# Maxima and u turned in 32x32 blocks on VectorE, u stored by SyncE, and a tail with another order and early loads

## The chip, the cores and the metric

One core of a Trainium2 chip runs the whole program. The metric is the device time in microseconds (us). The engines named here are TensorE (PE in the rows; its weight loads are PEld), VectorE (DVE), ScalarE (ACT), GpSimd (POOL) and SyncE (SP), which only issues transfers. Each works through its own list of instructions in order, and waits on semaphores that the others raise.

## The reference

A layer of a perceiver on 32 batches of 64 tokens with 128 features. Cross attention over a context of 1601 rows per batch, causal self attention over the tokens of a batch, and a gated feed-forward part with quantised weights and activations:

```python
# cross attention: 16 heads of 64, per batch b
qh = rms_norm(layernorm(x) @ Wq); kh = rms_norm(ctx @ Wk)
scores = where(arange(1601) < len[b], qh @ kh.T / sqrt(64), -1e9)
x = x + (softmax(scores) @ (ctx @ Wv)) @ Wo
# self attention: 16 heads of 64, causal mask (64 tokens lie within the global part of the mask)
x = x + (softmax(q @ k.T / sqrt(64)) @ v) @ w_out
# feed-forward, with the largest magnitude of whole tensors as quantisation scales
x = x + qdq(silu(qdq(z @ Wg.T)) * qdq(z @ Wu.T)) @ qdq(Wd).T
```

## The kernel before

**Three parts in a row.** `cross_attention` (to 2188 us in the profile), `self_attention` (to 2477) and `ffn`. A barrier of all engines lies between two parts.

**Cross attention.** The queries are first carried through Wk, so that a score is a product of the query with the raw context; the keys are still computed, for their norms. Then comes a loop over batches p, each of 13 steps c, one per tile of 128 context rows (the last has 65). `each_step` writes the steps out for the first and last batches and as a hardware loop between; `draining(p)` is p >= 32, where no new batch begins. One step of TensorE is: `project` (keys of a tile 11 ahead, for the sum of squares), `turn` (a transpose of the raw tile 12 ahead into the PSUM bank x_ps), `score` (two halves), `values` (tile of an earlier batch, LAG steps behind, times its probabilities, into u_ps), and at the end of some steps transposes that belong to a batch as a whole.

**Maxima.** VectorE keeps `best`, the maximum over the 13 score tiles element by element (128 x 1024, `keep_best`, not in step 1). When a batch is whole, the maximum over the 128 partitions is wanted, as one row of 1024. TensorE turns `best` in two groups of four 128x128 transposes (`turn_best`, end of steps 0 and 1), VectorE reduces each group from PSUM (`best_of_columns`, steps 1 and 2), TensorE turns the result (`turn_row`, step 2), ScalarE copies it (`save_row`, step 3), SyncE stores it to DRAM as `best_rows` and loads it back broadcast to all partitions as `best_all` (`spread_best`, step 6 of SyncE's own list, which runs about three steps ahead of TensorE). GpSimd subtracts it from the scores (`shift`), ScalarE exponentiates.

**u.** When all 13 tiles of values are summed, VectorE inverts the sums of probabilities (`invert_sums`, step LAG), ScalarE divides (`divide`), TensorE turns the result in two groups of four (`turn_u`, end of steps 7 and 8), ScalarE copies each group out of x_ps (`save_uT`) and issues one transfer of 128 rows of 4 KB to the DRAM tensor ut (`store_uT`).

**Stage.** Raw context tiles are loaded into `stage`, four buffers and one for the short tile, by SyncE (`load_stage`), each when the tile before it in its buffer has been turned. SyncE's transfers go through one queue in the order in which they are issued.

**Self attention.** STEPS run from -10 to 15, one token tile of 128 (two batches) per step, with five stages at different leads: `sum_heads` (tile i+10, 64 small products of u with Wv Wo, from the transfer `load_u` of 1 MB per tile into two buffers), `turn_y` (tile i+9), `project_qk` (part of the q and k projections, a group of four tiles in four steps, i from -5 to 10), `project_v`, `score`, and `turn_p`, `mix` for tile i. Of VectorE's work the chain for y is: add, variance, (ScalarE: rough root), `normalise`, then, when TensorE has turned y and ScalarE has copied it, yT_lo = y - yT_hi. The feed-forward weights are quantised by VectorE in one piece at step -6.

Of the kernel before, what the change touches and what calls it, by code (L numbers as in the profile page):

```python
# [110 lines left out]
def arena_views(arena):  # L111

    def at(first, count):
        return arena[:, first * HL:(first + count) * HL]

    return {"wqkv": at(0, 3), "wv": at(3, 1), "wo": at(4, 1), "wout": at(5, 1), "wvo": at(6, 2), "wvo2": at(8, 2),
            "wvT": at(10, 1), "wv2T": at(11, 1), "qk": [at(10, 8), at(18, 8)], "v2": [at(0, 2), at(2, 2)],
            "pT": at(4, 1), "p": at(5, 1)}
# [22 lines left out]
LAG = 6  # L141
# [42 lines left out]
def cross_attention(nc, sem, ident, x, ctx_in, Wq, Wk, q_norm_w, k_norm_w, lens, qs, best_rows, ut_out,  # L184
                    arena, Wv, Wo, w_qkv, w_out):
# [11 lines left out]
    UW = D + 1  # L197
    with ExitStack() as ctx:
# [20 lines left out]
        best_row = sb("best_row", [P, G])  # L219
        row_sb = sb("row_sb", [G, P])  # L220
# [46 lines left out]
        q_in, rows_in, ut_stored = sem("q_in"), sem("rows_in"), Turns(sem("ut_stored"), 1, 16)  # L267
# [19 lines left out]
        best_turned = Turns(sem("best_turned"), 2, 2)  # L287
        best_row_ready = Turns(sem("best_row_ready"), 2, 2)
        row_turned = Turns(sem("row_turned"), 2)
# [3 lines left out]
        last_spread, last_best_ready = sem("last_spread"), sem("last_best_ready")  # L293
# [4 lines left out]
        u_turned = Turns(sem("u_turned"), 2, 2)  # L298
        uT_ready = Turns(sem("uT_ready"), 2, 2)
# [14 lines left out]
        def _(sp):  # L314
# [29 lines left out]
            def spread_best(b):  # L344
                sp.wait_ge(row_saved.sem, row_saved.ended(b))
                sp.dma_start(best_rows[bass.ds(b, 1), :].rearrange("b (g p) -> (b g) p", p=P),
# [31 lines left out]

            row_stored.start(sp)
# [12 lines left out]
            sp.wait_ge(ut_stored.sem, ut_stored.ended(B - 1))  # L392
# [64 lines left out]
        def _(act):  # L457
# [95 lines left out]
            def save_row(b):  # L553
                act.wait_ge(row_turned.sem, row_turned.ended(b))
                act.wait_ge(row_stored.sem, row_stored.ended(b - 1))
                act.activation(row_sb[:, :], x_ps[0:G, 0:P], ACT.Copy).then_inc(row_saved.sem, 1)

            def save_last_best(b):
                for h in range(2):
                    act.wait_ge(last_spread, h + 1)  # L560
                    act.activation(best_all[:, (b % 2) * HL + h * HALF:(b % 2) * HL + (h + 1) * HALF], k_ps[h][:, :],
                                   ACT.Copy).then_inc(last_best_ready, 1)

            def divide(b):
                for k in range(3):
# [7 lines left out]
            def save_uT(b, h):  # L573
                act.wait_ge(u_turned.sem, u_turned.ended(b, h + 1))
                act.wait_ge(ut_stored.sem, ut_stored.ended(b - 1))
                act.activation(uT_sb[:, half(h)], x_ps[:, :], ACT.Copy).then_inc(uT_ready.sem, 1)  # L576

            def store_uT(b):
                act.wait_ge(uT_ready.sem, uT_ready.ended(b))
                act.dma_start(ut_out[bass.ds(b, 1), :, :].rearrange("b d n -> (b d) n"),  # L580
                              uT_sb[:, :]).then_inc(ut_stored.sem, 16)
# [39 lines left out]
            for turns in (hi_ready, squared, logged, y0_ready, probs_ready, row_saved, u_ready, uT_ready,  # L621
                          ut_stored, q_hi_ready):
# [1115 lines left out]
```

## Time and profile before

| | us |
|---|---|
| median of 3 runs (2638.5 to 2650.76) | 2642.37 |
| the profiled execution | 2639.05 |
| its span, first to last instruction | 2637.3 |

| stretch, us | what | TensorE busy | VectorE busy | clock granted |
|---|---|---|---|---|
| 0 to 151 | queries, first tiles | 116.25 | 97.00 | 0.93 |
| 151 to 2128 | loop over batches | 1957.83 | 1692.01 | 1.00 |
| 2128 to 2188.5 | drain, weight products | 49.10 | 31.86 | 0.97 |
| 2188.5 to 2477 | self attention | 234.85 | 140.69 | 0.90 |
| 2477 to 2637.3 | feed-forward | 68.38 | 104.25 | 0.72 |

A row of the timeline gives the start in us, the duration, engine, line of the kernel, operation, output and inputs; in brackets stands the idle time of that engine before it and what ended it. Matmuls overlap, so the distance between two starts tells more than a duration. The clock is TensorE's, as a share of 2.4 GHz.

### The profile page before, as it was taken

To read this page: it belongs to the slowest core of one execution; us is meant where nothing else is said; L and a number is where in the kernel's file an instruction comes from. 1 tells how busy PE (TensorE), PEld (TensorE's weight loads), DVE (VectorE), ACT (ScalarE), POOL (GpSimd) and SP (SyncE) were. 2 spreads that over 40 slices of the span, in tenths; PEclk is the share of its full clock that TensorE was granted. 3 is DMA by queue.
4 is the path that set the end of the run, shared out by engine and by line. 5 is a ranking of instruction groups with operands and counts; after the bars stand their busy time and mean duration, and the time that the engine had idled before them with its cause. 6 is when DMAs were issued, how large, how long until landed. Compare 5 with 4: busy or idle time off the path is not lost. (4 is left out here: it accounts for less than half of the span.)

```text
span 2637.3 us, 54923 instructions
## 1 busy us (share of the span) xinstructions
PE 2426.4 (92%) x17271; PEld 2036.6 (77%) x17271; DVE 2065.8 (78%) x3185; ACT 1333.0 (51%) x2659; POOL 1168.1 (44%) x605
## 2 busy tenths in 40 slices
PE   6879999999999999999999999999999986788852
PEld 3657888888888888888888888888888886565522
DVE  6789888888888888888888888888888863355757
ACT  4644555555555555555555555555555542334540
POOL 3403555555555555555555555555555510001155
PEclk8999999999999999999999999999999998988975
DMA  2421111111111211111111111111111115210000
GB/s 86 160 100 43 50 50 52 55 54 54 49 50 51 60 50 50 49 58 50 49 50 50 49 49 50 49 58 50 57 50 50 45 65 173 69 50 1 2 0 16
DMA packets 141723, 144.97 MB, mean 55 GB/s; under 512 B 10520, under 2 KB 120272, under 8 KB 141520
## 3 DMA queue, kind: packets, MB, share of 16 engines
q1 hardware_dynamic: 137040, 127.16, 15.3%
q10 hardware_dynamic: 4608, 16.78, 1.6%
q8 instruction: 51, 0.84, 0.1%
q14 instruction: 24, 0.20, 0.0%
HBM read 109.17 MB, written 34.73 MB: 55 GB/s over the span
## 5 line engine op out<-in xcount | busy, mean ns | idle before, releaser
L404 POOL TENSOR_TENSOR probs<-arena,best_all 128x1024 f32 (+2 forms) x398 | 944.9, 2377 | 918.9 <-DVE best L765 918.9
L984 PEld LDWEIGHTS u_ps<-rows,probs 128*128 128x128 f32 x6656 | 806.5, 192 | 47.1 <-issue 5.3
L984 PE MATMUL u_ps<-rows,probs 128*128 (+1 forms) x6656 | 810.1, 275 | 9.0 <-ACT probs L597 6.6
L750 DVE SCALAR_TENSOR_TENSOR arena<-s_ps,mask,rrms 128x512 f32 (+2 forms) x832 | 618.8, 745 | 249.6 <-PE s_ps L853 249.4
L597 ACT ACTIVATE probs<-probs 128x1024 f32<-128x1024 f32 (+1 forms) x416 | 439.6, 1058 | 512.9 <-POOL probs L404 501.5
L550 ACT ACTIVATE squares<-k_ps 128x512 f32<-128x512 f32 (+1 forms) x832 | 462.8, 595 | 191.4 <-PE k_ps L853 128.0
L726 DVE TENSOR_REDUCE ssq<-squares 128x16 f32<-128x1024 f32 (+1 forms) x416 | 502.4, 1208 | 0.0
L765 DVE TENSOR_TENSOR best<-best,arena 128x1024 f32<-128x1024 f32 (+1 forms) x352 | 468.9, 1332 | 0.3
L851 PE MATMUL k_ps<-w_hi,cT_hi 128*128 128x512 f32 (+1 forms) x832 | 363.2, 437 | 12.9 <-DVE cT_lo L720 12.9
L851 PE MATMUL s_ps<-q_hi,cT_hi 128*128 (+2 forms) x832 | 362.0, 435 | 2.5 <-ACT uT_sb L576 1.4
L853 PE MATMUL s_ps<-q_hi,cT_lo 128*128 (+2 forms) x832 | 327.8, 394 | 0.0
L853 PE MATMUL k_ps<-w_hi,cT_lo 128*128 128x512 f32 (+1 forms) x832 | 327.6, 394 | 0.0
L852 PE MATMUL s_ps<-q_lo,cT_hi 128*128 (+2 forms) x832 | 327.6, 394 | 0.0
L852 PE MATMUL k_ps<-w_lo,cT_hi 128*128 128x512 f32 (+1 forms) x832 | 326.9, 393 | 0.0
L851 PEld LDWEIGHTS s_ps<-q_hi,cT_hi 128*128 128x128 f32 (+1 forms) x832 | 153.6, 185 | 59.8 <-ACT uT_sb L576 1.9
L851 PEld LDWEIGHTS k_ps<-w_hi,cT_hi 128*128 128x128 f32 (+1 forms) x832 | 154.1, 185 | 41.7 <-DVE cT_lo L720 19.9
L853 PEld LDWEIGHTS k_ps<-w_hi,cT_lo 128*128 128x128 f32 (+1 forms) x832 | 152.9, 184 | 39.5
L853 PEld LDWEIGHTS s_ps<-q_hi,cT_lo 128*128 128x128 f32 (+1 forms) x832 | 152.8, 184 | 39.4
L852 PEld LDWEIGHTS k_ps<-w_lo,cT_hi 128*128 128x128 f32 (+1 forms) x832 | 154.5, 186 | 19.9
L852 PEld LDWEIGHTS s_ps<-q_lo,cT_hi 128*128 128x128 f32 (+1 forms) x832 | 154.3, 186 | 20.0
L720 DVE TENSOR_TENSOR cT_lo<-x_ps,cT_hi 128x128 fp32r<-128x128 f32 (+1 forms) x416 | 114.8, 276 | 45.2 <-ACT cT_hi L544 45.2
L576 ACT ACTIVATE uT_sb<-x_ps 128x512 f32<-128x512 f32 x64 | 38.4, 599 | 154.1 <-PE x_ps L970 154.1
(222 smaller groups left out, 2312.8 us busy)
## 6 DMA issues: line engine op xcount, KB each, us to landing
stage<-in_ctx SPq DMA_DIRECT2D x384, 64.0 KB, 1.8
rows<-in_ctx SPq DMA_DIRECT2D x32, 768.0 KB
queries<-probs SPq DMA_DIRECT2D x16, 1024.0 KB, 4.0
q_plain<-queries SPq DMA_DIRECT2D x32, 512.0 KB, 3.4
u_transposed<-uT_sb ACTq DMA_DIRECT2D x32, 512.0 KB, 2.7
a_uT<-u_transposed SPq DMA_DIRECT2D x16, 1024.0 KB, 4.9
best_all<-best_rows SPq DMA_DIRECT2D x31, 512.0 KB, 3.6
arena<-in_L_attn_w_qkv SPq DMA_DIRECT2D x1, 1536.0 KB, 6.6
```

The source lines that it names most:

```text
L404: pool.tensor_tensor(probs[0:r, slot_of(c, PRING), :], scores_at(b, c), best_all[0:r, bass.ds((b % 2) * HL, HL)], ALU.subtract).then_inc(s ...
L550: act.activation(squares[0:rows_of(c), half(h)], k_ps[h][0:rows_of(c), :], ACT.Square).then_inc(squared.sem, 1)
L576: act.activation(uT_sb[:, half(h)], x_ps[:, :], ACT.Copy).then_inc(uT_ready.sem, 1)
L597: act.activation(tile, tile, ACT.Exp).then_inc(probs_ready.sem, 1)
L720: dve.tensor_tensor(cT_lo[:, c, 0:r], x_ps[:, 0:r], cT_hi[:, c, 0:r], ALU.subtract).then_inc(lo_ready.sem, 1)
L726: dve.tensor_reduce(ssq[0:r, c * H:(c + 1) * H], squares[0:r, :].rearrange("p (h d) -> p h d", d=HD), AX_X, ALU.add).then_inc(summed.sem, 1)
L750: dve.scalar_tensor_tensor(out=scores_at(p, c, h * HALF, HALF).rearrange("p (h l) -> p h l", l=L), in0=s_ps[h][0:r, :].rearrange("p (h l) ...
L765: dve.tensor_tensor(best[0:r, :], so_far, scores_at(p, c), ALU.max).then_inc(kept.sem, 1)
L851: pe.matmul(out, cT_hi[:, c, 0:r], hi, start=True, stop=False)
L852: pe.matmul(out, cT_hi[:, c, 0:r], lo, start=False, stop=False)
L853: return pe.matmul(out, cT_lo[:, c, 0:r], hi, start=False, stop=True)
L984: last = pe.matmul(u_ps[g // 3][:, at:at + UW], probs[0:r, s, g * P:(g + 1) * P], rows, start=(c == 0 and g % 3 == 0), stop=(c == NC - 1), ...
```

## The change

In the loop, VectorE transposes `best` in 32x32 blocks into u_sb (`turn_blocks`, end of step 1), reduces each block's rows (`best_of_blocks`, steps 2 and 3, from SBUF, 128x32 results), TensorE turns the result at the end of step 4, and VectorE reduces the four rows groups of that from PSUM into `row_sb` of 32x32 (`best_of_groups`, step 5). TensorE's groups for `best` and ScalarE's `save_row` are gone. u is transposed in 32x32 blocks by VectorE too (`turn_u`, a quarter of 128x256 in each of four steps); blocks then lie in the wrong place, and SyncE's store puts them right: four transfers, each of 32 partitions x 32 pieces of 32 numbers (128 B). The last batch keeps the old way for both (`turn_last_best`, `turn_last_u`). LAG goes from 6 to 7.

In the tail, six u tiles (U_EARLY) are loaded into the finished half of the score buffer during the drain; `project_qk` waits only for the group's own tiles and takes the whole wait before its fourth product; `sum_heads` waits for one copy less of each kind; VectorE makes yT_lo before it normalises the next tile; the weights are quantised in three parts, at steps -7, -6 and -5.

```diff
-LAG = 6
+LAG = 7
+SIDE = 32
+            def store_uT(b):
+                sp.wait_ge(uT_ready.sem, uT_ready.ended(b))
+                dest = ut_out[bass.ds(b, 1), :, :].rearrange("b (c i) (g q k) -> b q i g c k", i=SIDE, k=SIDE, q=P // SIDE)
+                for q in range(P // SIDE):
+                    sp.dma_start(dest[:, q, :, :, :, :].rearrange("b i g c k -> (b i) g c k"),
+                                 uT_sb[q * SIDE:(q + 1) * SIDE, :].rearrange("i (g c k) -> i g c k", k=SIDE, c=D // SIDE)
+                                 ).then_inc(ut_stored.sem, 16)
+            def load_u_early(t):
+                sp.wait_ge(shifted.sem, shifted.ended((B - 1) * NC + 2 * t + 1))
+                if t == 0:
+                    sp.wait_ge(ut_stored.sem, ut_stored.ended(2 * U_EARLY - 1))
+                else:
+                    sp.wait_ge(u_early_in, 16 * t)
+                load_u(sp, w_now["uT"][t], ut_out, t, u_early_in)
 # SyncE's step
+                if c == NC - 1 and on.finish and not ending(p):
+                    store_uT(p - 2)
+                if draining(p) and (p - B) * NC + c in range(9, 9 + 2 * U_EARLY, 2):
+                    load_u_early(((p - B) * NC + c - 9) // 2)
 # ScalarE
             def divide(b):
+                act.wait_ge(uT_ready.sem, uT_ready.ended(b - 1))
+                act.wait_ge(best_row_ready.sem, best_row_ready.ended(min(b + 1, B - 2) if isinstance(b, int) else b + 1))
-                if on.rows and c == 3 and not draining(p):
-                    save_row(p - 1)
-                if on.finish and c in (LAG + 2, LAG + 3):
-                    save_uT(p - 2, c - LAG - 2)
-                if on.finish and c == LAG + 4:
-                    store_uT(p - 2)
 # VectorE
+            def turn_blocks(b):
+                dve.wait_ge(kept.sem, kept.ended(b))
+                dve.wait_ge(uT_ready.sem, uT_ready.ended(b - 2))
+                dve.transpose(u_sb[:, :], best[:, :]).then_inc(blocks_turned.sem, 1)
+            def best_of_blocks(b, h):
+                ...
+                dve.tensor_reduce(best_row[:, cols], u_sb[:, half(h)].rearrange("p (j k) -> p j k", k=SIDE),
+                                  AX_X, ALU.max).then_inc(best_row_ready.sem, 1)
+            def best_of_groups(b):
+                dve.wait_ge(row_turned.sem, row_turned.ended(b))
+                dve.wait_ge(row_stored.sem, row_stored.ended(b - 1))
+                dve.tensor_reduce(row_sb[:, :], x_ps[0:BLOCKS, 0:P].rearrange("j (g i) -> j i g", i=SIDE),
+                                  AX_X, ALU.max).then_inc(row_saved.sem, 1)
+            def turn_u(b, k):
+                if k == 0:
+                    dve.wait_ge(u_ready.sem, u_ready.ended(b))
+                    dve.wait_ge(ut_stored.sem, ut_stored.ended(b - 1))
+                cols = slice(k * HL // 4, (k + 1) * HL // 4)
+                dve.transpose(uT_sb[:, cols], u_sb[:, cols]).then_inc(uT_ready.sem, 1)
 # TensorE's step
-                if on.rows and c in (0, 1) and not draining(p):
-                    turn_best(p - 1, c)
-                if on.rows and c == 2 and not draining(p):
+                if on.rows and c == 4 and not draining(p):
                     turn_row(p - 1)
-                if on.finish and c in (LAG + 1, LAG + 2):
-                    turn_u(p - 2, c - LAG - 1)
+                if c in (LAG + 1, LAG + 2) and ending(p):
+                    turn_last_u(p - 2, c - LAG - 1)
 # tail: SyncE, VectorE, TensorE
-            load_u(0)
             sp.dma_start(x1[:, :].rearrange("p (t d) -> p t d", d=D),
                          x.rearrange("b l d -> (b l) d").rearrange("(t p) d -> p t d", p=P)).then_inc(x_in, 16)
-            load_u(1)
+            for t in range(U_EARLY, U_EARLY + 2):
+                load_u(sp, uT[:, t % 2, :], ut, t, uT_in[t % 2])
-                if i == -6:
-                    dve.wait_ge(ffn_w_in, 48)
-                    quantize_weights(dve, link, ffn_w, ws, ffn_w_ready)
+                if -7 <= i < -4:
+                    if i == -7:
+                        dve.wait_ge(ffn_w_in, 48)
+                    quantize_weights(dve, link, ffn_w, ws, i + 7, ffn_w_ready)
-                pe.wait_ge(v_saved, 4 * upto(i - 1, V_AHEAD))
-                pe.wait_ge(qk_saved, parts_upto(i - 1))
+                pe.wait_ge(v_saved, max(0, 4 * upto(i - 1, V_AHEAD) - 1))
+                pe.wait_ge(qk_saved, max(0, parts_upto(i - 1) - 1))
             def project_qk(j, r, i):
-                pe.wait_ge(yT_lo_ready, upto(i, TURN_Y_AHEAD))
+                pe.wait_ge(yT_lo_ready, 4 * j + 4)
...
+                    if k == 3:
+                        pe.wait_ge(yT_lo_ready, upto(i, TURN_Y_AHEAD))
```

What this does to the order of instructions, at three places. First VectorE in step 1 of a batch and the start of step 2 (written-out part); best is the running maximum, ssq the sums of squares, ms their mean, x_ps the bank that TensorE turns into. Before:

```order
L750 SCALAR_TENSOR_TENSOR arena<-s_ps,mask,rrms 128x512
L726 TENSOR_REDUCE ssq<-squares 65x16
L732 TENSOR_SCALAR ms<-ssq 128x64
L770 TENSOR_REDUCE best_row<-x_ps 128x4
L765 TENSOR_TENSOR best<-arena 128x1024
```

And of the change:

```order
L780 SCALAR_TENSOR_TENSOR arena<-s_ps,mask,rrms 128x512
L756 TENSOR_REDUCE ssq<-squares 65x16
L800 STREAM_TRANSPOSE u_sb<-best 128x1024
L762 TENSOR_SCALAR ms<-ssq 128x64
L795 TENSOR_TENSOR best<-arena 128x1024
```

The reduction from x_ps has gone from the start of step 2, and the block transpose of the whole maximum stands at the end of step 1, ahead of the next batch's first maximum.

Second SyncE at the end of the loop's body, from the load of tile 11 on; the branch goes back to the load of the next batch's tile 0. Before:

```order
L318 DMA stage<-in_ctx 128x128
L317 REGISTER_ALU
L318 ISA [waits turned]
L318 DMA stage<-in_ctx 65x128
L161 REGISTER_ALU
L161 COMPARE_AND_BRANCH
```

And of the change:

```order
L333 DMA stage<-in_ctx 65x128
L369 ISA
L372 ISA [waits uT_ready]
L372 DMA u_transposed<-uT_sb 256x4x32
L372 ISA
L372 DMA u_transposed<-uT_sb 256x4x32
L372 ISA
L372 DMA u_transposed<-uT_sb 256x4x32
L372 ISA
L372 DMA u_transposed<-uT_sb 256x4x32
L175 REGISTER_ALU
L175 COMPARE_AND_BRANCH
```

A wait for VectorE's last quarter of uT and four transfers stand ahead of the loads of the next batch's tiles.

Third VectorE in a tail step, from the sums of the softmax on (a_inv) to the sum with the attention's output (x<-a_ov). Before:

```order
L1291 RECIPROCAL a_inv<-a_total 128x16 [waits a_normed,a_links]
L1266 TENSOR_TENSOR a_y_stat<-a_y_stat 128x1 [waits a_y_rough,a_y_turned]
L1267 SCALAR_TENSOR_TENSOR a_y_stat<-a_y_stat 128x1 [waits a_links]
L1268 SCALAR_TENSOR_TENSOR a_y_stat<-a_y_stat 128x1 [waits a_links]
L1269 TENSOR_SCALAR a_y<-x_then_z,a_y_stat 128x128 [waits a_links]
L1320 TENSOR_TENSOR a_yT_lo<-a_work,a_yT_hi 128x128 [waits a_yT_ready]
L1324 TENSOR_TENSOR x<-a_ov,x_then_z 128x128 [waits a_mixed]
```

And of the change:

```order
L1346 RECIPROCAL a_inv<-a_total 128x16 [waits a_normed,a_links]
L1367 TENSOR_TENSOR a_yT_lo<-a_work,a_yT_hi 128x128 [waits a_yT_ready]
L1321 TENSOR_TENSOR a_y_stat<-a_y_stat 128x1 [waits a_y_rough,a_y_turned]
L1322 SCALAR_TENSOR_TENSOR a_y_stat<-a_y_stat 128x1 [waits a_links]
L1323 SCALAR_TENSOR_TENSOR a_y_stat<-a_y_stat 128x1 [waits a_links]
L1324 TENSOR_SCALAR a_y<-x_then_z,a_y_stat 128x128 [waits a_links]
L1380 TENSOR_TENSOR x<-a_ov,x_then_z 128x128 [waits a_mixed]
```

a_yT_lo, which the projection of q and k waits for, now comes before the four instructions that normalise the next tile.

## Rows read from the trace of the kernel before

**Rows 1.** Busy time by stretch: core, then as headed (the clock is PEclk).

```profile
core 0: us, PE busy (x) PEld busy (x) DVE busy (x) ACT busy (x) POOL busy (x), PEclk, DMA share, GB/s
1000.00:2060.00 1060.00, 1060.00 (x6663) 925.96 (x6662) 902.31 (x1305) 580.15 (x1148) 560.61 (x236) 1.00 0.16 51
...
2320.00:2340.00 20.00, 16.93 (x230) 12.01 (x229) 10.62 (x25) 8.06 (x17) 1.91 (x1) 0.84 0.16 53
...
2440.00:2460.00 20.00, 19.41 (x271) 12.00 (x264) 12.94 (x31) 12.66 (x26) 3.80 (x2) 1.00 0.01 2
```

**Rows 2.** Timeline of TensorE in the loop; stage is turned in step 1 of two batches.

```profile
1009.94 1.95 PE L984 MATMUL u_ps<-rows,probs 128*128 x16
...
1011.64 0.48 PE L851 MATMUL k_ps<-w_hi,cT_hi 128*128 128x512 f32 x1
...
1014.62 1.95 PE L984 MATMUL u_ps<-rows,probs 128*128 x16
...
1016.76 0.48 PE L851 MATMUL k_ps<-w_hi,cT_hi 128*65 128x512 f32 x1
...
1018.23 0.27 PE L926 MATMUL x_ps<-ident,stage 128*128 128x128 f32 x1
...
1080.97 0.27 PE L926 MATMUL x_ps<-ident,stage 128*128 128x128 f32 x1
```

**Rows 3.** Timeline of VectorE in the loop: end of step 11; steps 4 to 6.

```profile
1006.55 1.21 DVE L726 TENSOR_REDUCE ssq<-squares 128x16 f32<-128x1024 f32 x1
...
1036.61 1.21 DVE L765 TENSOR_TENSOR best<-best,arena 128x1024 f32<-128x1024 f32 x1
...
1038.63 0.75 DVE L750 SCALAR_TENSOR_TENSOR arena<-s_ps,mask,rrms 128x512 f32 x1 [0.81 <-PE s_ps L853]
```

**Rows 4.** Timeline of the transfers that SyncE issues.

```profile
1029.17 0.32 SPq L346 DMA_DIRECT2D best_rows<-row_sb  x1
...
1030.83 0.35 SPq L350 DMA_DIRECT2D best_all<-best_rows  x1
...
1043.36 0.40 SPq L366 DMA_DIRECT2D rows<-in_ctx  x1
```

**Rows 5.** Timeline of GpSimd: its first subtraction of a batch.

```profile
1038.30 2.38 POOL L404 TENSOR_TENSOR probs<-arena,best_all 128x1024 f32 x1 [2.59 <-DVE best L765]
```

**Rows 6.** Busy time by stretch, amid the load of rows1; last: DMA share, GB/s.

```profile
1046.25:1046.50 0.25, 0.25 (x3) 0.21 (x2) 0.25 (x1) 0.18 (x1) 0.00 (x0) 1.00 1.16 352
```

**Rows 7.** The page, part 6: transfers, count, KB each, median us to landing.

```profile
u_transposed<-uT_sb ACTq DMA_DIRECT2D x32, 512.0 KB, 2.7
...
best_all<-best_rows SPq DMA_DIRECT2D x31, 512.0 KB, 3.6
```

**Rows 8.** Timeline of TensorE in the tail.

```profile
2193.46 6.31 PE L1356 MATMUL a_work<-arena,a_uT 128*64 128x128 f32 x64 [6.16 <-DMA a_uT<-u_transposed]
...
2225.64 0.30 PE L1381 MATMUL a_work<-ident,a_y 128*128 128x128 f32 x1 [3.46 <-DVE a_yT_lo L1320]
...
2241.03 0.50 PE L1394 MATMUL a_tp<-a_yT_hi,a_wqk_hi 128*128 128x512 f32 x1 [2.69 <-DVE a_yT_lo L1320]
...
2244.97 3.71 PE L1356 MATMUL a_work<-arena,a_uT 128*64 128x128 f32 x64 [0.89 <-ACT arena L1240]
...
2251.63 0.50 PE L1394 MATMUL a_tp<-a_yT_hi,a_wqk_hi 128*128 128x512 f32 x1 [2.69 <-DVE a_yT_lo L1320]
...
2339.53 0.80 PE L1394 MATMUL a_tp<-a_yT_hi,a_wqk_hi 128*128 128x512 f32 x1 [3.07 <-DVE a_yT_lo L1320]
...
2359.91 0.80 PE L1394 MATMUL a_tp<-a_yT_hi,a_wqk_hi 128*128 128x512 f32 x1 [3.08 <-DVE a_yT_lo L1320]
...
2440.07 0.50 PE L1394 MATMUL a_tp<-a_yT_hi,a_wqk_hi 128*128 128x512 f32 x1
...
2451.04 0.50 PE L1394 MATMUL a_tp<-a_yT_hi,a_wqk_hi 128*128 128x512 f32 x1
```

**Rows 9.** Waits, 2188 to 2460 us: us in total, times, longest.

```profile
PE a_tp L1394 <- DVE a_yT_lo L1320: 37.7, 12, 5.3
```

More of the change, by code:

```diff
@@ L117, in arena_views, with load_u, ending @@
             "wvT": at(10, 1), "wv2T": at(11, 1), "qk": [at(10, 8), at(18, 8)], "v2": [at(0, 2), at(2, 2)],
-            "pT": at(4, 1), "p": at(5, 1)}
+            "pT": at(4, 1), "p": at(5, 1), "uT": [at(NC + 2 * t, 2) for t in range(U_EARLY)]}
+U_EARLY = 6
+def load_u(sp, dest, ut, t, done):
+    sp.dma_start(dest.rearrange("p (b n) -> p b n", b=2), ut[2 * t:2 * t + 2, :, :].rearrange("b d n -> d b n")).then_inc(done, 16)
+def ending(p):
+    return isinstance(p, int) and p == B + 1
 class On:
@@ L620, in _ @@
             act.preload_act_table_set(EXP_LN)
[L621 to L622 removed]
+            for turns in (hi_ready, squared, logged, y0_ready, probs_ready, u_ready, q_hi_ready):
                 turns.start(act)
@@ L790, in step @@
                 n = p * NC + c
-                if on.rows and c in (1, 2) and not draining(p):
-                    best_of_columns(p - 1, c - 1)
+                if on.rows and c == 5 and not draining(p):
+                    best_of_groups(p - 1)
                 if on.rows and c == 1 and draining(p):
@@ L811, in step @@
                     sum_squares(n + KEYS_AHEAD, at_step(p, c, KEYS_AHEAD)[1])
+                if on.rows and c == 1 and not draining(p):
+                    turn_blocks(p - 1)
+                if on.rows and c in (2, 3) and not draining(p):
+                    best_of_blocks(p - 1, c - 2)
+                if on.finish and LAG < c <= LAG + 4 and not ending(p):
+                    turn_u(p - 2, c - LAG - 1)
                 if on.early and c == NC - 3:
@@ L833, in save_wvo @@
                                         ).then_inc(wvo_saved, 1)
-            for turns in (lo_ready, summed, ms_ready, rrms_ready, scaled, kept, best_row_ready, inv_ready):
+            for turns in (lo_ready, summed, ms_ready, rrms_ready, scaled, kept, blocks_turned, best_row_ready, row_saved,
+                          inv_ready, uT_ready):
                 turns.start(dve)
@@ L1015, in step @@
                     project(n + KEYS_AHEAD, at_step(p, c, KEYS_AHEAD)[1])
-                if on.rows and c in (1, 2) and not draining(p):
-                    pe.wait_ge(best_row_ready.sem, best_row_ready.ended(p - 1, c))
-                if on.rows and c == 3 and not draining(p):
+                if on.rows and c == 5 and not draining(p):
                     pe.wait_ge(row_saved.sem, row_saved.ended(p - 1))
-                if on.finish and c in (LAG + 2, LAG + 3):
-                    pe.wait_ge(uT_ready.sem, uT_ready.ended(p - 2, c - LAG - 1))
+                if c == LAG + 2 and ending(p):
+                    pe.wait_ge(last_saved, 3)
                 if on.turn:
@@ L1041, in step @@
                     spread_last_best(p - 1)
-                if on.finish and c in (LAG + 1, LAG + 2):
-                    turn_u(p - 2, c - LAG - 1)
-            for turns in (turned, keys, scored, valued, best_turned, row_turned, u_turned):
+                if c in (LAG + 1, LAG + 2) and ending(p):
+                    turn_last_u(p - 2, c - LAG - 1)
+            for turns in (turned, keys, scored, valued, row_turned):
                 turns.start(pe)
@@ L1187, in _ @@
             sp.dma_start(ffn_w[:, 2 * FF:3 * FF], w_down).then_inc(ffn_w_in, 16)
-            for t in range(2, TILES):
-                load_u(t)
+            for t in range(U_EARLY + 2, TILES):
+                sp.wait_ge(summed, t - 1)
+                load_u(sp, uT[:, t % 2, :], ut, t, uT_in[t % 2])
         @block.gpsimd
@@ L1310, in step @@
                     softmax_sums(t)
+                t = i + TURN_Y_AHEAD
+                if 0 <= t < TILES:
+                    dve.wait_ge(yT_ready, t + 1)
+                    at = t % 8 * P
+                    dve.tensor_tensor(yT_lo[:, at:at + P], work[1][:, 0:P], yT_hi[:, at:at + P], ALU.subtract).then_inc(yT_lo_ready, 1)
                 t = i + SUM_AHEAD
```

139 lines of the change are left out of this document (71 added, 68 removed).

## The prediction

> **What bounds the kernel now.** I read the busy time by stretch first, then the timelines of TensorE and VectorE inside the loop, then the tail's timeline and its waits. In 1000 to 2060 us TensorE is busy for all of it, at a granted clock of 1.00 (2.4 GHz), while VectorE has 902 of 1060 us and GpSimd 561 [rows 1]. VectorE is the one that waits, as for the 0.81 us before the scores at 1038.63 [rows 3]. So the loop over batches costs what TensorE is given, 62.74 us per batch (1018.23 to 1080.97, the same turn of the same tile) [rows 2]. The tail is different: at 2320 to 2340 the clock is 0.84, at 2440 to 2460 it is 1.00 [rows 1], and in the first TensorE stands still for 3.07 us in every step before projecting q and k, waiting for VectorE's yT_lo [rows 8]; 12 such waits make 37.7 us [rows 9].
>
> **The change, part by part, the loop.** TensorE loses four groups of four transposes per batch (maxima in steps 0 and 1, u in steps 7 and 8); the single turn of the row stays. Without a group the time from a step's values to the next projection is 1.70 us (1009.94 to 1011.64), with one it is 2.14 (1014.62 to 1016.76) [rows 2]: 0.44 us each, all on the path, since TensorE waits for nothing there. The maxima of 31 batches are turned so (the last batch's stay on TensorE), 62 groups; u has as many, of which the last two lie in the drain, where TensorE is not the bound, and I leave those out: 60. 122 x 0.44 = 53.7 us less.
>
> VectorE gains, per batch, a block transpose of 128x1024, four of 128x256 and a small reduction of 32x128; two PSUM reductions of 128x512 become two in SBUF, which I price alike. No row shows a transpose on VectorE. From above I bound the large one by 2.38 us, what GpSimd needs over 1024 columns [rows 5]; from below by the 0.75 us that VectorE needs over 512 [rows 3]. I take 1.2, by its reduction and its maximum over 1024 columns (1.21 us each [rows 3]), and 0.3 for a quarter. That adds 1.2 + 4 x 0.3 + 0.2 = 2.6 us to 902 / 1060 of 62.74 = 53.4; 56.0 of the new 61.0 fit (62.74 - 4 x 0.44 = 60.98). So it stays off the path only if the work lies evenly. Step by step: after a plain step VectorE is done at 1037.82 and waits 0.81 us for the next scores [rows 3], so a step gives back 0.8 us of lateness. Step 1 has no maximum and takes most of the large transpose free. By adding up, step 2 starts its scaling 0.4 us late, then holds a reduction and the refinement; step 3 starts about 1.0 late. TensorE wants cT_lo, which comes behind the first scaling, about 1.0 us after it is normally there (an estimate from the order of the two timelines). I book 0.1 us per batch, none to 1.0.
>
> A second small one: maxima now reach the row in step 5, not 3. Today the row's store is issued at 1029.17, the broadcast at 1030.83 [rows 4], and it lands 3.6 us later [rows 7], near 1034.4; GpSimd first uses it at 1038.30 [rows 5]. In the new order it is stored about 1.6 us into step 5, so lands 5.3 us after that, some 2.3 us into step 6, where GpSimd (now a step later) wants it at 2.2. ScalarE's exponential, its division and then cT_hi sit behind that chain. I book 0.2, none to 1.0 where the row's 32 pieces are slower than its 8. Together 0.3 x 31 = 9 us more; with a transpose of twice the price, about 1.5 x 31 = 47.
>
> **The store of u.** SyncE writes it as four transfers of 1024 pieces of 128 B instead of one of 128 rows of 4 KB. They stand ahead of the next three stage loads on its queue, and SyncE itself waits for the last transpose there. The first of those loads used to have three steps in hand. VectorE's sum of step 11 ends at 1007.76 [rows 3]; with a quarter transpose and some lateness uT is whole near 1008.5, pieces move from about 1009.7 (an estimate: 1.1 us or so behind the issue, as the load of rows1 issued at 1043.36 was under way well before 1046.25). The tile is turned at 1018.23 less one removed group, 1017.8, and I allow 1 us behind the last piece, so the 4096 pieces have 7.1 us, 1.73 ns each [rows 2, 4, 6]. Price of a piece: no row has it. Pieces of 512 B moved at 352 GB/s in that load [rows 6], 1.45 ns each, 6.0 us in all. By bytes alone it would be 2.7, the landing time of the old store [rows 7]. Upwards the rows give no end (the row's store, 8 pieces in 1.66 us, is all latency [rows 4]), and I cap it at two 512 B pieces per piece, 12.0 us. I take 6.0 to 7.5, by the nearest row, and book nothing; at the cap the stall is 4.9 us per batch, 150 us.
>
> The Trainium skill (DMA: Bandwidth & Descriptors, Specifications) speaks against this edit: it puts the least transfer for line rate at 512 B and says that below it the engine reads, modifies and writes. By that rule a piece pays for two passes, and with the second rival's length the sum would be its 2680. No row of this trace shows such a store, and the sum above goes by the row.
>
> **The tail.** Six of the sixteen u tiles are loaded while the drain runs. Today TensorE waits 6.16 us for the first and then works slowly; step 0's add falls about 6 us earlier, bounded now by x, which moves to the front of the queue. Quantising the weights in one piece kept TensorE for 3.46 us (2225.64); in thirds behind the normalisation it still delays two adds by about 1.3 us each. With the wait for yT_lo and the slow clock of that step I get 6.5 us. Then the wait itself: three of four projections need only tiles turned a step earlier, and take 2.1 us at full clock; yT_lo now comes before the normalisation, so by adding up it is there about 2.5 us after the sum of heads, when the fourth wants it. Steps with all parts take 20.4 us (2339.53 to 2359.91). Steps without y and without a wait take 10.97 (2440.07 to 2451.04); adding the sum of heads (3.7) gives 14.7, and with the turn of y and the smaller pauses I keep 14.6 to 15. Six such steps: 35 us. The two steps of 10.6 (2241.03 to 2251.63) go to 6.9: 7. Three others (before, between and after) about 5 each: 15. All: 6 + 6.5 + 35 + 7 + 15 = 70 us [rows 8]. 36 of these are the waits, most of the rest is the clock: behind the pause the projection's row has 0.80 us (2339.53), where it has 0.50 without one (2440.07). If the clock stays low regardless only about 48 come. I take 60. VectorE has 10.6 us of work in 20 [rows 1], one step; that fits 14.6.
>
> LAG 7 moves one tile of values out of the loop into the drain, where it takes as long as it did; early loads share the queue with u's store. I book 0, +-5.
>
> **Sum.** The profiled execution took 2639.05 us (span 2637.3 and 1.75 around it): 2639.05 - 53.7 + 9 - 60 = 2534. The median of the runs shown is 3.3 above it, so 2538.
>
> **Rivals.** (1) The store is somewhat slower than the queue allows, 1.8 to 2.6 ns a piece: a stall of 0.3 to 3.6 us in each of 30 batches, 2545 to 2640. For it: writes, scattered, in four transfers; against: a piece carries a quarter of the bytes of the row that I price it by. Chance 0.23. (2) The other side: the same mechanism beyond 3.7 us per batch (decided at 2.65 ns a piece, since 53.7 + 60 - 9 = 105 us is what must be used up with the drain; at 12.0 us of transfer, 4.9 x 30 = 147) gives about 2680, slower. TensorE would show the wait at the stage's turn in step 1. Chance 0.15. (3) VectorE becomes the bound: a transpose of twice the price, or blocking with GpSimd, 1.5 us per batch, 2538 + 38 = 2576, up to 2600. For it: VectorE's small reserve; against: the transposes come 2.7 us after the maxima, when GpSimd's 2.38 us are over. Chance 0.15. (4) The tail does not do what it says, because another semaphore holds the projection: 2538 + 50 = 2588. Chance 0.05. Forecast: 0.42.
>
> **Numbers.** 2538 us. Its own range is 2515 to 2560; with (1), (3) and (4) it becomes 2512 to 2635, leaving out case (2) and little at the lower edge. Within 0.5% is 2629 to 2656, about what a measurement of this kernel can tell from no change; it gets the upper edge of (1) and the lower of (2), 0.05. Faster 0.82, slower 0.13.
>
> **What would show it.** A period of 61.0 to 61.5 us between the same turns; no TensorE wait for a stage load; a block transpose of 1.1 to 1.3 us; the store landing in under 9 us; in the tail steps of about 14.6 us at a clock near 1.00, with yT_lo waits below 1 us. A period above 62.7, or a wait of TensorE on the stage, makes it wrong; a tail step that keeps a 3 us pause makes that term wrong.

## The result, and the profile after

The changed kernel takes 2530.51 us (median of 4 runs, 2528.97 to 2531.81), the kernel before 2641.75 beside it: a ratio of 0.9573, 95% interval 0.9549 to 0.9598. 2538 was forecast, with 2512 to 2635 as the range. Single executions of 4165 to 8387 us, which came up beside the rest with the kernel before as with changed ones, are left out of every ratio.

The profiled executions have spans of 2637.3 and 2527.2 us, so 110.1 us went. A short tile is the last one of a batch, with 65 rows; TensorE turns one in each batch. Cut at the same instructions in both timelines, the 110.1 us went here:

| stretch | before | after | less |
|---|---|---|---|
| start to the first turn of a short tile | 150.67 | 149.58 | 1.1 |
| from there to the last tile's key projection (2083.16, 2039.60) | 1932.49 | 1890.02 | 42.5 |
| from there to the end of the weight products (2187.30, 2139.48) | 104.14 | 99.88 | 4.3 |
| from there to the sum of heads of step -5 (2218.47, 2169.24) | 31.17 | 29.76 | 1.4 |
| steps -5 to 0 (to 2291.14, 2217.87) | 72.67 | 48.63 | 24.0 |
| steps 0 to 5 (to 2391.83, 2289.16) | 100.69 | 71.29 | 29.4 |
| from there to the end | 245.5 | 238.0 | 7.4 |

Busy time by stretch, of the changed kernel; it answers to [rows 1]. Columns are as there.

```profile
1000.00:2060.00 1060.00, 1057.13 (x6533) 914.82 (x6532) 968.48 (x1435) 566.20 (x1114) 575.61 (x243) 1.00 0.20 51
2232.12:2246.38 14.26, 14.26 (x230) 10.39 (x230) 10.85 (x26) 7.73 (x18) 1.90 (x1) 1.00 0.22 76
```

In the loop TensorE is still busy nearly all the time, VectorE has 968 us instead of 902. The second row is one full step of the tail: 14.26 us, TensorE never idle, the granted clock 1.00, where it stood at 0.84 in 2320 to 2340 before. Five full steps (0 to 5) as a whole, before and then after:

```profile
2291.14:2391.83 100.69, 85.32 (x1147) 60.09 (x1146) 53.64 (x126) 40.32 (x86) 9.53 (x5) 0.85 0.13 43
```

```profile
2217.87:2289.16 71.29, 71.29 (x1146) 51.95 (x1146) 54.26 (x126) 38.67 (x86) 9.53 (x5) 1.00 0.18 61
```

In steps -5 to 0 TensorE had 50.42 us of work in 72.67, at a clock of 0.91, and has 45.60 in 48.63 at 1.00. So of the 53.4 us that went in steps -5 to 5, 34.6 were time in which TensorE stood idle, and 18.8 are the same products done faster.

TensorE in the loop, against [rows 2]: stage turned in step 1 of two batches, and in steps 7 and 8 between them.

```profile
1061.23 0.27 PE L988 MATMUL x_ps<-ident,stage 128*128 128x128 f32 x1
...
1089.53 0.27 PE L988 MATMUL x_ps<-ident,stage 128*128 128x128 f32 x1
...
1094.57 0.27 PE L988 MATMUL x_ps<-ident,stage 128*128 128x128 f32 x1
...
1122.61 0.27 PE L988 MATMUL x_ps<-ident,stage 128*128 128x128 f32 x1
```

The period here is 61.38 us. From short tile to short tile the 29 whole periods run from 61.10 to 61.53, mean 61.26, where before they ran from 62.70 to 62.76, mean 62.73 (62.74 in the rows). The unevenness is new, and the rows show one place of it: 5.04 us from step 7 to step 8. Averaged over 20 batches, the time from the turn of one step to the turn of the next is:

| step | 0 | 1 | 2 | 3 | 4 | 5 | 6 | 7 | 8 | 9 to 12 |
|---|---|---|---|---|---|---|---|---|---|---|
| before | 5.11 | 5.10 | 4.79 | 4.67 | 4.69 | 4.69 | 4.75 | 5.12 | 5.10 | 4.67 to 4.69 |
| after | 4.69 | 4.67 | 4.67 | 4.68 | 4.80 | 4.80 | 4.69 | 4.88 | 4.67 | 4.67 to 4.69 |

A plain step takes 4.67. The four groups are gone whole (0.43 each). The 0.12 in step 4 is the turn of the row, which stood in step 2 before; what the new order costs stands in steps 5 (0.11) and 7 (0.20), and step 6 gives 0.06 back.

VectorE's new instructions: engine, count, ns min/median/max, first and last start (two lines of the source).

```profile
L800 DVE STREAM_TRANSPOSE u_sb<-best x31: 1229/1231/1236, 209.0 to 2044.5; 128x1024 f32<-128x1024 f32 x31
...
L826 DVE STREAM_TRANSPOSE uT_sb<-u_sb x124: 425/435/440, 301.8 to 2113.4; 128x256 f32<-128x256 f32 x124
```

The store of u, against [rows 4, 6, 7]: SyncE's issues, then two stretches of the share of the queue (last: DMA share, GB/s), then the page's part 6.

```profile
1052.18 3.01 SPq L372 DMA_DIRECT2D u_transposed<-uT_sb  x4
1055.73 2.08 SPq L333 DMA_DIRECT2D stage<-in_ctx  x4
```

```profile
1053.00:1053.50 0.50, 0.50 (x4) 0.36 (x3) 0.50 (x1) 0.50 (x2) 0.00 (x0) 1.00 0.01 1
...
1053.50:1055.50 2.00, 2.00 (x19) 1.95 (x18) 2.00 (x5) 0.37 (x2) 1.24 (x1) 1.00 0.98 169
```

```profile
best_all<-best_rows SPq DMA_DIRECT2D x31, 512.0 KB, 3.8
u_transposed<-uT_sb SPq DMA_DIRECT2D x124, 128.0 KB, 2.5
```

The pieces start 1.3 us behind the first issue and fill the 16 engines at 169 GB/s, so the 524 KB take 3.1 us: 0.76 ns for a piece of 128 B. They are over near 1056.6, and the tile that comes first behind them is turned at 1061.23 without a wait. The old store, rows of 4 KB in the same direction, ran at 394 GB/s once under way:

```profile
1026.60:1027.40 0.80, 0.80 (x6) 0.68 (x5) 0.77 (x3) 0.38 (x2) 0.10 (x1) 1.00 0.96 394
```

TensorE in the tail, against [rows 8]: the sums of heads of steps -10, -9 and 1, and the fourth product of two steps.

```profile
2140.96 3.71 PE L1417 MATMUL a_work<-arena 128*64 128x128 f32 x64 [1.48 <-PEq L213]
2148.54 6.15 PE L1417 MATMUL a_work<-arena 128*64 128x128 f32 x64 [3.87 <-DVEq L1358]
...
2211.28 0.50 PE L1457 MATMUL a_work<-a_yT_hi,a_wqk_hi 128*128 128x512 f32 x1 [0.77 <-DVE a_yT_lo L1367]
...
2232.12 3.71 PE L1417 MATMUL a_work<-arena,a_uT 128*64 128x128 f32 x64
...
2309.22 0.50 PE L1457 MATMUL a_work<-a_yT_hi,a_wqk_hi 128*128 128x512 f32 x1 [1.08 <-DVE a_yT_lo L1367]
```

And TensorE's waits in 2140 to 2400, us in total, times, longest; the last of these answers to [rows 9].

```profile
PE a_work L1417 <- DVEq L1358: 6.2, 5, 3.9
...
PE a_work L1457 <- DVE a_yT_lo L1367: 2.8, 3, 1.1
```

37.7 us of waits for yT_lo have become 2.8. What is left at the front is the add of x (L1358 of VectorE) that the second sum of heads waits for.

### The profile page after: what moved, and what is told of

It reads as the page before. It is cut to its first block and busy times, and to the rows that moved or that the text cites. A ratio compares the mean times of both kernels' runs of the same rounds, so it can differ in the third digit from the quotient of the medians.

```text
span 2527.2 us, 54183 instructions
## 1 busy us (share of the span) xinstructions
PE 2358.9 (93%) x16775; PEld 1966.5 (78%) x16775; DVE 2149.5 (85%) x3384; ACT 1282.4 (51%) x2566; POOL 1165.3 (46%) x604
## 5 line engine op out<-in xcount | busy, mean ns | idle before, releaser
L586 ACT ACTIVATE squares<-k_ps 128x512 f32<-128x512 f32 (+1 forms) x832 | 455.4, 591 | 126.2 <-PE k_ps L915 67.0
L795 DVE TENSOR_TENSOR best<-best,arena 128x1024 f32<-128x1024 f32 (+1 forms) x352 | 475.6, 1351 | 0.1
L580 ACT ACTIVATE cT_hi<-x_ps 128x128 fp32r<-128x128 f32 (+1 forms) x416 | 115.5, 278 | 0.0
```

The lines of the kernel that those rows point to most:

```text
L580: act.activation(cT_hi[:, c, 0:rows_of(c)], x_ps[:, 0:rows_of(c)], ACT.Copy).then_inc(hi_ready.sem, 1)
L586: act.activation(squares[0:rows_of(c), half(h)], k_ps[h][0:rows_of(c), :], ACT.Square).then_inc(squared.sem, 1)
L795: dve.tensor_tensor(best[0:r, :], so_far, scores_at(p, c), ALU.max).then_inc(kept.sem, 1)
```

## The experiments

Each is the changed kernel with one edit, or with those that its heading names. The time from the start to the first short tile is between 149.2 and 159.0 us in these profiles, with the same code there, so small effects are read as the time between two instructions, not from the medians alone.

**1. The tail as it was, the loop changed** (all the tail's hunks of the diff undone).

> The changed kernel with the tail as it was: whole wait for yT_lo ahead of the projection, yT_lo behind the normalisation, weights quantised in one piece, no early loads of u, sum_heads' waits as before. The loop keeps its change. Theory (the two parts add up): from the end of the weight products to the end of the program the traces differ by 62 us (450.0 against 387.7), so this kernel takes 2530.5 + 62 = 2593 us, steps of 20.4 us in the tail. Rival (early loads and the loop's stores of u disturb each other, so that part of the tail's gain is used up in the loop or the drain): clearly under 2593, 2580 or less.

Measured 2593.65 us; ratio to before 0.9815, 0.9787 to 0.9843. The loop alone is worth 47.5 us (2641.19 beside it), the tail 63.1, and they add up. Steps 1 to 3 take 20.37 to 20.45 us again.

**2. The wait alone.**

```diff
 def project_qk(j, r, i):
-                pe.wait_ge(yT_lo_ready, 4 * j + 4)
+                pe.wait_ge(yT_lo_ready, upto(i, TURN_Y_AHEAD))
```

> The changed kernel, only the projection of q and k waits for the newest yT_lo ahead of its first product instead of ahead of its fourth. Theory: in a full step yT_lo is there at 2238.8 where the projection begins at 2237.76, so TensorE waits 1.1 us in each of some 11 steps: 12 to 13 us, 2543, if only the wait itself counts. Rival (the granted clock falls behind such a pause, as it stood at 0.84 in the old steps with their 3.07 us pause): steps of 17 us or more instead of 15.4, in all 30 us or more, 2560, and a clock below 0.95 in the steps 2240 to 2330.

Measured 2558.03 (2550.36 to 2565.2). Since the start varies, the time from the first sum of heads to the end is surer: 413.6 us against 386.2, 27.4 more. Busy time of this kernel in steps -5 to 0 and 0 to 5:

```profile
2242.79:2319.79 77.00, 72.70 (x1147) 52.30 (x1146) 54.26 (x126) 40.38 (x86) 9.53 (x5) 1.00 0.16 57
...
2178.24:2242.79 64.55, 51.48 (x554) 38.23 (x554) 23.43 (x73) 22.56 (x54) 1.91 (x1) 0.89 0.19 66
```

Both theories hold, each in its part. In the full steps TensorE stands still for 0.86 us a step, each costs 1.14 us (15.40 against 14.26), and the clock stays at 1.00. In steps -5 to 0, where TensorE had 51.48 of 64.55 us of work, the clock is 0.89, and these five steps cost 15.9 us more: 10.0 in which TensorE is idle, and 5.9 because the same 554 products take 51.48 us and not 45.60. Another 5.8 us stand in the last full step and the one behind it, at a clock of 0.88.

**3. VectorE's order alone**: yT_lo behind `normalise` again.

> The changed kernel, only VectorE normalises the next tile of y before it makes yT_lo, as it did before; the narrow wait stays. Theory: the normalisation takes 2.4 us of VectorE (2238.72 to 2241.1), so yT_lo comes at about 2241.1 where the fourth product stands at 2239.9: 1.2 us per step, 11 steps, 13 us, 2544. Rival (the fourth product has slack because of ScalarE's copies that project_v waits for, so that the order alone costs nothing): 2531 to 2534. Rival with the clock: as for the front wait, 2560.

Measured 2545.57 (2543.38 to 2548.51), and 398.9 us from the first sum of heads, 12.7 more. The theory's 13 as a sum, with full steps of 15.56 us at a clock of 1.00. They do not lie evenly, as the theory had them: a full step costs 1.3 us, step -1 costs 4.05 by itself, and steps -5 to -2 together 0.8.

**4. Both.**

> The changed kernel with both the old wait and the old order on VectorE, the rest of the tail as changed. Theory: the two hide each other's gain: the wait is 1.1 + 2.4 = 3.5 us a step, more than the sum of both alone, and the clock falls: steps of about 20 us, so 2530.5 + 50 = 2580. Rival (waits only, the clock stays near 1.00): 11 x 3.5 = 38, 2569.

Measured 2587.54; from the first sum of heads 442.6 us, 56.3 more, where the two alone make 40.1. The same two stretches of this kernel:

```profile
2239.40:2338.72 99.32, 83.96 (x1146) 59.34 (x1146) 53.64 (x126) 40.33 (x86) 9.53 (x5) 0.86 0.13 44
...
2170.61:2239.40 68.79, 51.09 (x554) 38.07 (x554) 23.43 (x73) 22.53 (x54) 1.90 (x1) 0.88 0.18 62
```

Now the clock is down in the full steps too: the same 1146 products take 83.96 us of TensorE, where they take 72.70 in experiment 2 and 71.29 in the changed kernel. Waits of 12 times 3.2 us make 38.7 of the 56; the rest goes with the clock.

**5. The weights quantised in one piece**, at step -6.

> The changed kernel with the feed-forward weights quantised in one piece at step -6, ahead of the sums of the softmax, as before. Theory (the prediction's term of 6.5 us; of the two kernels with the old wait and the old order, that with one piece takes 59.2 us from the sum of heads of step -6 to that of step -2 without its own wait for x, that with three parts 53.5 or so): 6 us are lost, 2536, and they stand in the steps -6 to -3. Rival (with the narrow wait the projection no longer needs yT_lo at once, so VectorE's block delays only the adds): 2 us, 2532.

Measured 2531.77 (2531.01 to 2533.79): the rival. Step -5 takes 12.78 us against 8.71, step -6 4.25 against 5.53, and the steps behind them are equal. With the narrow wait the long block costs 2.8 us by these two steps (1.3 by the medians).

**6. No early loads of u** (U_EARLY = 0).

> The changed kernel without the six early loads of u (U_EARLY = 0); u and x are loaded behind the barrier in the old order. Theory (from two earlier traces: with early loads the first sum of heads comes 4.5 us sooner, but then TensorE stands for VectorE's add, which waits for x, and works through its first two tiles at a low clock; from the last turn of a short tile to the sum of heads of step -5 it is 132.8 us with and 134.4 without): 1.5 us are lost, 2532, inside what the medians can tell; in the trace 134 to 135 us between those two points. Rival (the prediction's term): 6 us are lost, 2537, 139 us between the points.

Measured 2534.59; between the two points 135.75 us (2038.75 to 2174.50) against 132.86 in the changed kernel: 2.9 us, nearer to the theory. TensorE waits 6.19 us for the first u tile, as before, but no longer for x behind it:

```profile
2148.45 5.99 PE L1417 MATMUL a_work<-arena,a_uT 128*64 128x128 f32 x64 [6.19 <-DMA a_uT<-u_transposed]
2156.00 3.71 PE L1417 MATMUL a_work<-arena,a_uT 128*64 128x128 f32 x64 [1.56 <-DMA a_uT<-u_transposed]
```

**7. Six tiles of x loaded early as well** (run with the edits of 12; a load into a free slot behind the wait of the first early u load, and VectorE's add reads it there).

> As the kernel before it, and the first six tiles of x loaded early too, into a free slot of the arena during the drain; the add of steps -10 to -5 reads them there. Theory (x is what bounds the tail's start: TensorE stands 3.87 us for the add, and the second tile's sum then takes 6.15 instead of 3.71 us at a low clock): from the end of the weight products to the sum of heads of step -5 it is 31.2 us in the changed kernel and becomes 25, 6 us less, 2512 to 2515. Rival (something else, such as the first u tile or the clock, holds the start as long): 30 us there and 2518 to 2521.

Measured 2517.65 (2515.34 to 2519.79), ratio to before 0.9531, 0.9514 to 0.9547. Its first two sums of heads:

```profile
2132.05 5.38 PE L1426 MATMUL a_work<-arena 128*64 128x128 f32 x64 [3.42 <-PEq L214]
2138.03 3.71 PE L1426 MATMUL a_work<-arena 128*64 128x128 f32 x64 [0.61 <-DVEq L1367]
```

The wait for the add went from 3.87 (4.32 in kernel 12) to 0.61 us, and the second sum is fast. But the first now stands 3.42 us behind TensorE's own sequencer and is slow. From the end of the weight products to step -5, where the theory had 31.2 us (this is the kernel before; the changed kernel has 29.8) and 25 with the early loads, it is 27.68 against 29.46 in kernel 12: 1.8 us, not 6. Another 1.3 us are missing from the drain ahead of it (129.86 against 132.94 from the last short tile's turn to step -5), but the drain varies by as much between kernels that have the same code there. From the first short tile to the end the two kernels differ by 1.1 us; most of the 5.1 us between the medians can be the start, which took 6.9 us longer in the profile of kernel 12. What the 3.42 us are, no run shows; the kernel of experiment 4, which loads no x early, has 2.81 us at the same place.

**8. The store of u issued twice** (the second time to a spare tensor), and **9. three times.**

```diff
+                for to in [dest] + [ut_spare[...] ...]:
                     for q in range(P // SIDE):
-                        sp.dma_start(dest[:, q, ...
+                        sp.dma_start(to[:, q, ...
```

> The changed kernel, every store of u issued twice in the loop (the second four transfers go to a spare tensor in DRAM), so SyncE moves 8192 pieces of 128 B ahead of the next stage loads. In the trace the 4096 pieces move from 1053.3 to about 1056.5, at 153 to 198 GB/s with the 16 engines full: 3.2 us, 0.77 ns a piece. Theory (the prediction's 7.1 us between the start of the pieces and 1 us ahead of the tile's turn): 6.4 us fit, 2530 to 2535. Rival (the reserve is smaller, as the loads behind the store are late already): 3 us per batch, 2620.

> The same with three stores, 12288 pieces. Theory: 9.6 us of transfer against 7.1, so a stall of 2.5 us in each of 30 batches, 75 us, 2605, with TensorE waiting for stage ahead of a turn in step 1. Rival (pieces of two stores overlap better, or later loads take up the delay from the ring of four buffers): under 2560. Rival (other transfers of the batch, rows1 and the row of maxima, are delayed as well): over 2640.

Twice: 2530.89 us (2527.79 to 2532.45), no difference. The queue in its loop:

```profile
1054.25:1060.25 6.00, 6.00 (x43) 5.38 (x43) 5.67 (x9) 2.45 (x6) 3.77 (x2) 1.00 1.02 174
```

At this rate the 8192 pieces (1049 KB) take 6.0 us, and they cost nothing, as 7.1 us of room says. Three times: 2646.34 (2638.06 to 2660.66), 116 us more, mean period 65.3. TensorE waits at the turn of step 1, as the second rival of the prediction had it:

```profile
1049.94 0.33 PE L989 MATMUL x_ps<-ident,stage 128*128 128x128 f32 x1 [2.71 <-DMA stage<-in_ctx]
```

The step ahead of this turn takes 7.63 us on average instead of 4.69, the one behind it 6.04 instead of 4.67. The second of these, 1.4 us, is what the expectation lacked: the next load was late too. So the end of the reserve lies between 6.0 us of transfer and the 9.3 us that 12288 pieces take at 0.76 ns. The wait grew by 2.95 us (7.63 less 4.69), which puts it near 6.4 us (an estimate: 9.3 less 2.95), and behind it a batch pays 4.0 us.

**10. The block transpose of the maxima made twice.**

> The changed kernel, the block transpose of the maxima made twice (the second waits for the first, same result): VectorE has 1.3 us more in step 1 of each batch. Theory (lateness step by step): cT_lo ends at 1068.45 in step 2 and the projection that wants it begins at 1069.11, in step 3 1073.48 against 1073.78; so 0.65 us are lost in step 2 and some 0.35 in step 3, 1.0 us per batch, 31 us, 2561. Rival (VectorE's free share, 5 us of 61, takes it): 2531. Rival (all of it is lost): 1.3 x 31 = 40, 2571.

Measured 2566.01 (2563.73 to 2566.69), 35.5 more. Step 2 takes 5.39 us (0.72 more), step 3 5.03 (0.35), step 4 4.95 (0.15), all others are equal. VectorE's reserve in these steps was about 0.1 us, although it is idle for 9% of the loop. The theory holds, 15% low.

**11. The turned row reduced ahead of the sum of squares**, in step 4 of VectorE.

```diff
-                if on.rows and c == 5 and not draining(p):
-                    best_of_groups(p - 1)
                 ...
+                if on.rows and c == 4 and not draining(p):
+                    best_of_groups(p - 1)
                 if on.keys:
                     sum_squares(...)
```

> The changed kernel, only VectorE reduces the turned row (best_of_groups) ahead of the sum of squares of step 4 instead of at the start of step 5. Theory (the period's 61.26 us are 13 x 4.67 = 60.71 and 0.12 for turning the row, 0.12 for TensorE's wait for the reduction in step 5, and 0.1 to 0.4 in step 7, where the broadcast of the row comes late and holds GpSimd, ScalarE's division, cT_hi, cT_lo and so the projection): both waits go, the period is 60.85 in nearly all batches, 0.4 x 31 = 12 us less, 2518. Rival (only the wait in step 5 goes): 2526. Rival (VectorE waits some 0.4 us for the row in step 4 and that delays the scaling behind it): 2531 or more.

Measured 2531.49 (2524.28 to 2538.89), period 61.13 to 61.26, mean 61.20. A miss. The theory had 60.85. Step 5 fell from 4.80 to 4.68, and GpSimd's waits for best_all (46.5 us in 20 of 21 batches of the changed kernel, 400 to 1700 us) are gone; but step 7 did not fall: it takes 4.95 where it took 4.88 (4.86 to 4.95 in the kernels above that leave the loop's order alone). GpSimd then waits for VectorE's maximum instead. ScalarE in step 7 of this kernel:

```profile
1094.34 1.06 ACT L628 ACTIVATE probs<-probs 128x1024 f32<-128x1024 f32 x1 [1.89 <-POOL probs L440]
1095.31 2.16 ACT L602 ACTIVATE u_sb<-u_ps,inv_sum 128x128 f32<-128x128 f32 x8
1097.31 1.14 ACT L586 ACTIVATE squares<-k_ps 128x512 f32<-128x512 f32 x2
1098.26 0.35 ACT L580 ACTIVATE cT_hi<-x_ps 128x128 fp32r<-128x128 f32 x1
```

The tile was turned at 1095.63, yet cT_hi is made at 1098.26, and the projection starts at 1099.08. So what bounds step 7 in this kernel is this chain on ScalarE, not when the row arrives. Experiment 12 tests it.

**12. The same, and cT_hi ahead of the squares in the step with the division.**

```diff
+                if on.turn and on.finish and c == LAG:
+                    split_hi(n + TURN_AHEAD, at_step(p, c, TURN_AHEAD)[1])
                 if on.keys:
                     for h in range(2):
                         square(...)
-                if on.turn:
+                if on.turn and not (on.finish and c == LAG):
                     split_hi(...)
```

> The changed kernel with the turned row reduced ahead of the sum of squares, and ScalarE copying cT_hi ahead of the squares in the step with the division. Theory (with the first edit alone step 7 still took 4.95 us, since behind the division's 2.16 us ScalarE makes the squares, 1.14, and only then cT_hi, which cT_lo and the next projection wait for): cT_hi comes 1 us earlier, step 7 falls to 4.68, the period from 61.20 to 60.95 or less, against 61.26 that is 9 to 13 us in all, 2518 to 2521. Rival (the squares come late instead, and the projection then waits for the banks k_ps that they read): the period stays at 61.15 to 61.2, 2529. The time from the start to the first short tile varies by some us from run to run, so the period is the surer reading.

Measured 2522.79 (2519.42 to 2525.63), ratio to before 0.9547, 0.9530 to 0.9563; each of its five runs is under the fastest of the changed kernel. ScalarE and TensorE of this kernel in the same step:

```profile
1090.39 2.15 ACT L602 ACTIVATE u_sb<-u_ps,inv_sum 128x128 f32<-128x128 f32 x8
1092.39 0.33 ACT L580 ACTIVATE cT_hi<-x_ps 128x128 fp32r<-128x128 f32 x1
1092.55 1.14 ACT L586 ACTIVATE squares<-k_ps 128x512 f32<-128x512 f32 x2
```

```profile
1090.69 0.27 PE L990 MATMUL x_ps<-ident,stage 128*128 128x128 f32 x1
...
1093.89 0.48 PE L915 MATMUL k_ps<-w_hi,cT_hi 128*128 128x512 f32 x1
```

From the turn to the next projection it is 3.20 us, where kernel 11 needed 3.45. Step 7 takes 4.68, the period is 60.88 to 60.96 in all 29 batches. Both kernels 12 and 7 beat the changed kernel, by 7.7 and 12.9 us in the medians, and by 9.9 and 11.0 from the first short tile to the end; 29 periods shorter by 0.34 make 9.9.

## Why the prediction was right

**TensorE's term, 53.7 us.** Right. A group cost 0.43 us in the table of steps (0.44 booked), and nothing took its place but the loop's losses, which come next.

**The loop's losses, 0.3 us per batch.** The size was right, the two reasons were not, so that the size came out is luck. The period fell by 62.73 - 61.26 = 1.47 us where four groups make 1.76, so the loss is 0.29. None of it is the lateness behind the large transpose, for which I booked 0.1: steps 2 and 3 take 4.67 and 4.68. Experiment 10 shows that this was close, since the next 1.3 us on VectorE are paid nearly in full, and so the upper bound of the term (1.5 us per batch for a transpose of twice the price) was well placed, at 1.2. The other 0.2, for the row that comes late to GpSimd, was seen as a wait (up to 2.6 us in the trace), but experiment 11 took that wait away and step 7 did not get shorter. What the table of steps shows is 0.11 in step 5 (the reduction ahead of cT_lo on VectorE) and 0.2 in step 7 (the division and the squares ahead of cT_hi on ScalarE). Experiments 11 and 12 took these away one after the other; ScalarE's order alone, with the row as late as it was, no run tried.

**The durations on VectorE.** 1.231 us for the large transpose, 1.2 taken. A quarter is 0.435, not 0.3: a part of a fourth of the columns does not take a fourth of the time. That is 0.5 us per batch of VectorE's time more than booked, in steps 8 to 11, where it cost nothing.

**The store of u, nothing booked.** Right in the sum, wrong in the price. I took 6.0 to 7.5 us, from pieces of 512 B; it is 3.1, half of that. The room of 7.1 us was somewhat too wide: by experiments 8 and 9 it ends nearer 6.4. So with the price that I took the store could have cost up to 1.1 us per batch, some 30 us in all; that it cost nothing rests on the price, which I had wrong. With 6.4 us of room rival (1) would have begun beyond 1.56 ns a piece (1.73 by the prediction's 7.1), where 0.76 was measured. The Trainium skill (DMA: Bandwidth & Descriptors, Specifications) has a read-modify-write below 512 B. The trace agrees that small pieces run below full rate: 169 GB/s for those of 128 B, 394 for the old store's rows of 4 KB, 352 for pieces of 512 B in a load. But a piece of 128 B takes half the time of one of 512 B, not two passes of it, and no row shows the read itself.

**The tail, 60 us.** 62.3 from the end of the weight products on, 63.1 by experiment 1. The parts booked made 69.5, and I had taken 60 in case the clock stays low. The clock came back whole, and the parts fell short in the start, so that 60 was close is partly luck. By parts, booked and measured: the six full steps 35, 34.1 (14.26 us each, 14.6 to 15 forecast); the two short ones 7, 6.4; three others 15, 14.1; the step with the quantising 6.5, 7.2; the start 6, 1.4. The start was mis-sized: loading u early moved TensorE's wait of 6.16 us to 1.48, but the add of x then held the second tile for 3.87 us and its products ran 2.4 us longer. Experiment 6 gives the early loads 2.9 us. Experiment 7 takes the wait for x away, but gains only 1.8 us of the 6 expected, so x is not all that bounds the start; what else does stays open. The quantising step's gain is right, but only 1.3 to 2.8 us of it is the splitting (experiment 5); the rest goes with the wait and the clock. That the steps' gain beside the waits is the clock is shown by the 18.8 us of TensorE's own time above, and by experiments 2 and 4, which bring the waits and the slow products back.

**The drain, 0.** 4.3 us went between the last key projection and the end of the weight products. Three of the 122 groups of transposes (1.3 us) and TensorE's waits for the engines that read them (0.78, 0.69 and 0.69 us in the timeline before, 2.2 in all) lay there. I had not counted these waits. The two groups of u that I had left out as off the path lay there too. The drain varies by up to 1.5 us between kernels with the same code there.

**The rivals.** (1) and (2) needed a slower store, (3) a slower VectorE, (4) another semaphore at the projection. None came, and experiments 8 to 10 show how far away the first three were: twice the store's time was free, VectorE had 0.1 us. A slip in (2) changes nothing here: 105 us over 30 batches are 3.5 us, not 3.7.

## What to carry to other kernels

Where one engine is busy throughout, look at the time from step to step for the steps that are longer than a plain one. That table named the place of both of the loop's losses here, while the waits named a transfer whose removal did not shorten the step. A free share of time on a second engine is no reserve: it is what is left in the step in which the work is put. And two changes that shorten the same wait are not priced by undoing each alone: the front wait cost 27.4 us, VectorE's order 12.7, both 56.3, since the pause went from 0.9 or 1.0 us a step to 3.1 and the clock fell with it.

## What the hardware did that was not expected

- Pieces of 128 B from 32 partitions to DRAM ran at 169 to 174 GB/s with the 16 engines full, 0.75 ns a piece, over 3 and over 6 us. SyncE needed 0.6 us to issue each transfer of 1024 pieces, and its issues followed each other at 0.75 to 0.80 us, about what 1024 pieces take. No run separates the two; the engines' share of 0.98 speaks for the pieces.
- A 32x32 block transpose on VectorE took 1231 ns for 128x1024 and 435 ns for 128x256 in fp32, with a spread under 4% in all instances.
- A pause of 0.9 us in each step of 15.4 us left the granted clock at 1.00 (2.4 GHz). With pauses of 3.1 us in steps of 20 it was 0.86, a mean of times at 2.4 and at 1.2 GHz, and the same products took 15% longer on TensorE.
- The same code took between 149.2 and 159.0 us from the start to the first short tile, from one profiled execution to the next, which is more than several of the effects measured here.
